# A graph layer on one core: x + beta divided between GpSimd and VectorE, the destination copy moved to ScalarE, a fused compare

## What is computed

```python
h = jnp.maximum(_layernorm(x, axis=-1), 0.0)
edge_input = jnp.concatenate([h[src], h[dst], edge_features, c[src][:, None], c[dst][:, None]], axis=-1)
messages = jax.nn.silu(edge_input @ mW1 + mb1) @ mW2 + mb2
aggregated = jax.ops.segment_sum(messages, dst, num_segments=n_nodes)
u = jax.nn.silu(jnp.concatenate([h, aggregated, c[:, None]], axis=-1) @ uW1 + ub1)
x = x + _layernorm(h + u @ uW2 + ub2, ln_gamma, ln_beta)     # c is node_vec
```

## Time and profile before

| what | us |
|---|---|
| runs | 715.4, 720.5, 722.17 |
| median | 720.5 |
| the profiled execution, its own time | 722.67 |
| span of its instructions | 720.8 |
| busy: PE, DVE | 630.0 (87%), 642.1 (89%) |
| busy: ACT, POOL | 516.5 (72%), 541.0 (75%) |

### The profile page before, as it was taken

How to read it: one execution, slowest core, us unless ns; L and a number is a source line. 1 busy time by engine, 2 the same in 40 slices (tenths; PEclk the granted TensorE clock), 3 DMA queues, 4 the chain that set the end, 5 groups by cost and what they waited for, 6 DMA issues and landing times.

```text
span 720.8 us, 17511 instructions
## 1 busy us (share of the span) xinstructions
PE 630.0 (87%) x3830; PEld 466.2 (65%) x3830; DVE 642.1 (89%) x3060; ACT 516.5 (72%) x1034; POOL 541.0 (75%) x448
## 2 busy tenths in 40 slices
PE   1468999999999999999998998998998998999981
PEld 0235676766776776766766766766767767767771
DVE  4365699999999999999999999999999999999897
ACT  1546778778877787787787787787788788788630
POOL 7778878888888888888888888888888888881210
PEclk9966999999999999999999999999999999999997
DMA  6445556666666666666765766756666766765231
GB/s 133 111 115 131 151 164 160 186 187 163 180 186 163 190 179 163 189 181 161 194 177 160 204 169 166 202 163 170 199 160 179 196 156 180 198 161 173 87 122 69
DMA packets 119053, 118.54 MB, mean 164 GB/s; under 512 B 48764, under 2 KB 93615, under 8 KB 119010
## 3 DMA queue, kind: packets, MB, share of 16 engines
q1 hardware_dynamic: 104884, 91.41, 43.6%
q0 software_dynamic: 12608, 26.25, 16.4%
q10 hardware_dynamic: 1518, 0.42, 0.3%
HBM read 79.31 MB, written 38.70 MB: 164 GB/s over the span
## 4 chain that ended last, share of the span: by engine, by line
POOL 60%; issue 21%; PE 8%; DVE 6%; ACT 2%; DMA 1%; POOLq 1%; ACTq 0%
POOL ends_in L373 47%; POOL x_beta L393 13%; ACT ends_norm L532 2%; DVE y_out L749 1%; DVE centred L632 1%; PE ps_e L458 1%; PE ps_t L486 1%; PE ps_hid L445 1%; PE ps_hid L447 1%; PE ps_e L457 1%; PE ps_e L456 1%; DVE stats L677 1%; PE ps_t L464 1%; DMA ends_in<-in_rows,end_idx 1%; PE ps_f L490 0%
## 5 line engine op out<-in xcount | busy, mean ns | idle before, releaser
L373 POOL DMA_INDIRECT ends_in<-in_rows,end_idx x392 | 422.6, 1078 | 113.3 <-issue 112.5
L476 PE MATMUL ps_upd<-w_out,hidden_n 128*128 128x128 f32 x784 | 140.4, 284 | 33.6 <-DVE centred L632 31.6
L532 ACT ACTIVATE ends_norm<-ends_in,minus,rstd 128x128 f32<-128x128 f32 x392 | 155.9, 484 | 6.6 <-DVE minus L743 6.6
L532 ACT ACTIVATE x_norm<-x_in,minus,rstd 128x128 f32<-128x128 f32 x392 | 156.0, 488 | 6.3 <-DVE minus L743 6.3
L476 PEld LDWEIGHTS ps_upd<-w_out,hidden_n 128*128 128x128 f32 x784 | 119.4, 192 | 41.9 <-DVE centred L632 26.4
L393 POOL TENSOR_TENSOR x_beta<-x_in,beta_row 128x1024 f32<-128x1024 f32 x49 | 116.0, 2368 | 39.1 <-DVE y_out L749 38.2
L632 DVE SCALAR_TENSOR_TENSOR centred<-ps_upd,y_mean,gamma_row 128x128 f32<-128x128 f32 x392 | 135.0, 347 | 0.1
L447 PEld LDWEIGHTS ps_hid<-match,msg_in 113*128 113x128 f32 x784 | 103.0, 191 | 47.2 <-issue 47.2
L537 ACT ACTIVATE ends_t<-ps_t 128x1024 f32<-128x1024 f32 x49 | 50.2, 1024 | 90.9 <-PE ps_f L490 89.3
L477 PE MATMUL ps_upd<-const_sb,h_t 128*128 128x128 f32 x392 | 107.6, 274 | 0.0
L749 DVE SCALAR_TENSOR_TENSOR y_out<-centred,rstd,x_beta 128x128 f32<-128x128 f32 x392 | 107.1, 348 | 0.0
(11 more groups left out here) (79 smaller groups left out, 885.7 us busy)
## 6 DMA issues: line engine op xcount, KB each, us to landing
x_in<-in_x_steps SPq DMA_DIRECT2D x49, 512.0 KB, 5.2
out<-y_out SPq DMA_DIRECT2D x49, 512.0 KB
msg_in<-msgs SPq DMA_DIRECT2D x392, 56.4 KB
msgs<-msg SPq DMA_DIRECT2D x49, 258.0 KB
ends_in<-in_rows,end_idx POOLq DMA_INDIRECT x392
ends_in<-in_attr SPq DMA_DIRECT2D x49, 64.0 KB
end_idx<-in_ends SPq DMA_DIRECT2D x49, 4.0 KB
match<-in_node_vec SPq DMA_DIRECT2D x49, 4.0 KB
```

The lines of the kernel that those rows point to most:

```text
L373: nc.gpsimd.indirect_dma_start(out=dst, out_offset=None, in_=rows, in_offset=bass.IndirectOffsetOnAxis(ap=end_idx[s.slot][:, t, side:side ...
L476: nc.tensor.matmul(ps_upd[:, cols(j)], hidden_n[:, cols(j)], w_out[:, :], start=j % E_TILES == 0, stop=False)
L532: return nc.scalar.activation(dst, source, function, bias=minus[was][:, c:c + 1], scale=rstd[was][:, c:c + 1])
```

## The change

1. `x_beta` is made in two parts: POOL adds tiles 0 to 4 (128x640), DVE adds tiles 5 to 7 (128x384) in the new `add_beta`, which stands between `rstd` and `minus`. Two semaphores take the place of one; SP and `y_out` wait for both.
2. `place` is gone. `match` is one scalar_tensor_tensor on a row of 1024 running numbers: (iota + block base) compared with the destination. The base is a scalar operand read per partition. `match` now stands behind `minus`, right ahead of `y_out`. The running numbers are 128x1024 in SBUF, loaded once, by a transfer on POOL's queue ahead of the first gather; the 128-column ramp in `consts` goes.
3. The polynomial of the Halley step is factored, so that `root_d` and one waited-for step go: 11 small operations in place of 12. `root_c` is a scalar_tensor_tensor with two tensor inputs in place of a tensor_scalar. The eviction of messages now stands behind `newton_b`.
4. The destination copy is an ACT activation between `hidden_e` and `h_t`.

```diff
+POOL_TILES = 5
...
-                nc.gpsimd.tensor_tensor(x_beta[near.slot][:, :, :], x_in[near.slot][:, :, :],
-                                        beta_row[:, :, :].broadcast_to([P, N_TILES, H]), ALU.add).then_inc(x_beta_ready, 1)
+                nc.gpsimd.tensor_tensor(x_beta[near.slot][:, 0:POOL_TILES, :], x_in[near.slot][:, 0:POOL_TILES, :],
+                                        beta_row[:, :, :].broadcast_to([P, POOL_TILES, H]), ALU.add).then_inc(x_beta_low_ready, 1)
...
+            pool.dma_start(iota[:, :, :].rearrange("p j m -> p (j m)"), iota_row.rearrange("(o n) -> o n", o=1).broadcast_to([P, N_STEP])).then_inc(iota_loaded, 16)
...
+                if own:
+                    act.wait_ge(edge_loaded[own.slot], (own.fills4 + 1) * 16)
+                    wait(act, msg_stored[own.slot], 16 * own.fills4)
+                    nc.scalar.activation(msg[own.slot][:, :, H:H + 1], end_idx[own.slot][:, :, 1:2], ACT.Copy).then_inc(dst_copied, 1)
...
-                    V.tensor_tensor(match[near.half][0:WINDOW, :, :], place[near.half][0:WINDOW, :, :].broadcast_to([WINDOW, N_TILES, P]),
-                                    iota[0:WINDOW, :, :].broadcast_to([WINDOW, N_TILES, P]), ALU.is_equal).then_inc(match_ready, 1)
+                    V.scalar_tensor_tensor(match[near.half][0:WINDOW, :, :], iota[0:WINDOW, :, :],
+                                           const[0:WINDOW, bass.ds(C_BASE + N_TILES * near.n, 1)],
+                                           msg_in[near.half][0:WINDOW, :, H:H + 1].broadcast_to([WINDOW, N_TILES, P]),
+                                           ALU.add, ALU.is_equal).then_inc(match_ready, 1)
...
+                def add_beta():
...
+                    wait(dve, out_ready, near.n - RING + 1)
...
+                    V.tensor_tensor(x_beta[near.slot][:, POOL_TILES:, :], x_in[near.slot][:, POOL_TILES:, :],
+                                    beta_row[:, :, :].broadcast_to([P, N_TILES - POOL_TILES, H]), ALU.add).then_inc(x_beta_high_ready, 1)
...
-                V.tensor_scalar(root_c[:, at], root_b[:, at], 0.375, -1.25, ALU.mult, ALU.add).then_inc(stat_ops, 1)
+                V.scalar_tensor_tensor(root_c[:, at], root_b[:, at], 10.0 / 3.0, root_b[:, at], ALU.subtract, ALU.mult).then_inc(stat_ops, 1)
...
-                V.tensor_tensor(root_d[:, at], root_c[:, at], root_b[:, at], ALU.mult).then_inc(stat_ops, 1)
+                V.scalar_tensor_tensor(halley[:, at], root_c[:, at], 5.0, guess[:, at], ALU.add, ALU.mult).then_inc(stat_ops, 1)
```

More of the change, by code:

```diff
@@ L46 @@
 MAGIC = 0x5F3759DF
-C_IDENT, C_LOWER, C_IOTA = 0, P, 2 * P
-C_BOUND = 3 * P
+C_IDENT, C_LOWER = 0, P
+C_BOUND = 2 * P
 C_SEARCH = C_BOUND + PER_LANE + 1
@@ L143, in gnn_layer @@
 def gnn_layer(nc, rows, x_steps, ends, dst_all, dst_seen, attr, node_vec, mW1, mb1, mW2, mb2, uW1, ub1, uW2, ub2,
-              gamma, beta, consts, out):
+              gamma, beta, consts, iota_row, out):
     f32, bf16, i32 = mybir.dt.float32, mybir.dt.bfloat16, mybir.dt.int32
@@ L203, in gnn_layer @@
         msg_in = [sb(f"msg_in{b}", [P, N_TILES, MSG_ROW]) for b in range(2)]
-        place = [sb(f"place{b}", [P, N_TILES, 1]) for b in range(2)]
+        iota = sb("iota_sb", [P, N_TILES, P])
         match = [sb(f"match{b}", [P, N_TILES, P]) for b in range(2)]
@@ L644, in evict_messages, with match_nodes @@
                                     fold_bias[:, :, :].broadcast_to([P, E_TILES, H]), ALU.add).then_inc(msg_ready, 1)
-                def copy_dst():
-                    if not own:
-                        return
-                    dve.wait_ge(edge_loaded[own.slot], (own.fills4 + 1) * 16)
-                    wait(dve, msg_stored[own.slot], 16 * own.fills4)
-                    V.tensor_copy(msg[own.slot][:, :, H:H + 1], end_idx[own.slot][:, :, 1:2]).then_inc(dst_copied, 1)
-                def place_messages():
+                def match_nodes():
                     if not near:
@@ L688, in body @@
                 if not (new or nxt or prev):
-                    copy_dst()
                     evict_messages()
-                    place_messages()
+                    add_beta()
                     match_nodes()
@@ L733, in body @@
                 evict_messages()
                 dve.wait_ge(stat_ops, base + 11)
-                V.scalar_tensor_tensor(newton_b[:, at], newton_a[:, at], -0.5, var[:, at], ALU.mult, ALU.mult).then_inc(stat_ops, 1)
-                place_messages()
-                dve.wait_ge(stat_ops, base + 12)
                 wait(dve, ends_norm_ready, it.edges_upto(-RING))
                 wait(dve, x_norm_ready, it.nodes_upto(-2))
-                V.scalar_tensor_tensor(rstd[b][:, at], newton_b[:, at], 1.5, halley[:, at], ALU.add, ALU.mult).then_inc(rstd_ready, 1)
@@ L741, in body @@
-                match_nodes()
+                V.scalar_tensor_tensor(rstd[b][:, at], newton_b[:, at], 1.5 * 0.375, halley[:, at], ALU.add, ALU.mult).then_inc(rstd_ready, 1)
+                add_beta()
                 dve.wait_ge(rstd_ready, 2 * it.stats_before() + 1)
                 V.scalar_tensor_tensor(minus[b][:, at], s_add[:, at], -0.5, rstd[b][:, at], ALU.mult, ALU.mult).then_inc(rstd_ready, 1)
+                match_nodes()
                 if prev:
                     dve.wait_ge(centred_ready, 2 * prev.n + 2)
-                    dve.wait_ge(x_beta_ready, prev.n + 1)
+                    dve.wait_ge(x_beta_low_ready, prev.n + 1)
+                    dve.wait_ge(x_beta_high_ready, prev.n + 1)
@@ L812 @@
               "uW1": L0_gnn_uW1, "ub1": L0_gnn_ub1, "uW2": L0_gnn_uW2, "ub2": L0_gnn_ub2,
-              "gamma": L0_gnn_ln_gamma, "beta": L0_gnn_ln_beta, "consts": consts}
+              "gamma": L0_gnn_ln_gamma, "beta": L0_gnn_ln_beta, "consts": consts, "iota": np.arange(N_STEP, dtype=np.float32)}
     nc = bacc.Bacc("TRN2", target_bir_lowering=False, num_devices=1)
```

31 lines of the change are left out of this document (14 added, 17 removed).

## The result

The changed kernel takes 732.9 us (median of 4, 731.1 to 734.5) where the kernel before takes 720.1: a ratio of 1.019, 95% interval 1.013 to 1.024. It is slower by nearly 2%. The interval lies above 1, so the loss is real. The forecast of 717 was wrong; the time is near that of the first rival (736). The profiled execution took 734.5 with a span of 732.5.

A forecast was written before the change was run, and what follows sets the result against it. The prediction took two bounds: a PE and ACT ring (13.2 us a period), then full POOL (13.42). With the ring setting all periods, -6.4 + 0.6 + 0.5 = -5.3 from 722.67 gave 717 us; range 712 to 742 for 8 in 10.

The forecast's parts named there:

- the first rival: DVE's hold on POOL runs through from `match` to the last `y_out`: slower, 736 us, about 775 if most gathers miss; chance 0.36.
- The ring of 13.20: Loop through PE and ACT, without DVE and POOL, claimed to set every one of 42 periods at 13.20 us: -6.4 us.
- POOL 11.42 without stretches: POOL's need per period in us without lengthened gathers, after its x_beta falls from 2.36 to 1.50.
- DVE: DVE's work per period: +0.18 us in sum, 12.85 without its wait for gathers, under the ring's 13.20.
- What POOL does in its spare time: POOL's add waits for `y_out`, so POOL rests there while `y_out` holds it up anyway; lengthened gathers cost nothing.
- the large stretch: The gather on POOL that takes 1.90 us in place of 0.95, held until 0.83 after the last `y_out`.
- The rival's price: A hold of 3.4 us costs POOL 2.15 to 3.4 a period; period taken as 13.7, +12.6 over 42 periods.
- The toss-up: Whether POOL's sixth gather slips in ahead of `match` or behind `add_beta` (13.6 us a period) or misses it (14.7).
- The dearer case: The sixth gather misses getting in ahead of `match`: periods of 14.7 us, about 775 in all; chance 0.05.
- ACT's copy: The destination copy on ACT fits the 0.52 us gap before `h_t`: cost 0, 0.12 left; rival 726 us, chance 0.05.
- Start and end: Ahead of the steady periods +0.6 us for one more load on POOL's queue; last iterations +0.5 us on DVE.
- The sum: All terms for the whole kernel: -6.4 + 0.6 + 0.5 = -5.3 us, from 722.67 to 717.4.

The follow-up runs named there:

- Kind 8: In a kernel without the layer: `match` directly ahead of eight `y_out` with two already met waits between; the gather ended 0.82 us after the last `y_out`.
- the good kernels: Changed kernel with `minus` between `match` and `y_out`, 714.8 us; kernel before with a 24-column copy inside `y_out`, 715.9; kernel before with x_beta's division alone, 716.3.
- The pairs: Kernel without the layer: POOL issues gathers, DVE runs 12 kinds of `match` then eight `y_out`, 9 times each; gathers came through between them in 54 of 108.
- the kernel with the order alone changed: Kernel before, loop in three stretches: `minus` ahead of `match`; as it was; a 24-column copy inside `y_out`. 745.1 us, ratio 1.034.
- the kernel with three stretches: Changed kernel, loop in three: as changed; old compare directly ahead of `y_out`; fused compare with `minus` between it and `y_out`. 727.5 us, ratio 1.009.
- kind 5: In a kernel without the layer: `match` directly ahead of eight `y_out` with a constant scalar; no gather came through between `match` and `y_out`.

## Why the prediction was wrong

- **The ring of 13.20**: right. The first six periods of the changed kernel have a mean of 13.18; with `minus` between, 36 of 42 are 13.18 to 13.20.
- **POOL 11.42 without stretches**: right. `x_beta` took 1.55, not 1.50; the period without stretches comes to 11.46.
- **DVE**: `add_beta` 0.47 from start to start (0.46 expected), the fused `match` 405.31 - 404.11 = 1.20 against 1.15, so +0.05 for +0.08. DVE did not set the period.
- **The step that failed** is "What POOL does in its spare time": that the large stretch falls into time that is free. It rested on a gather coming through between `match` and `y_out`, so that one period holds POOL for about one `y_out` row. The argument against the rival was that waits for semaphores between the two may open the gap. Kind 8 shows that met waits don't. What the runs showed in its place: the seventh gather, held through to the end of the last `y_out`, takes 2.99 to 3.09 us in nearly every period, so that POOL mostly needs 13.6 to 13.9, over the ring. The trace of before held the pattern already: between `match` and `minus` a gather came through each time (43 of 43), between one `y_out` and the next never (0 of 41). What was missing was to ask what distinguishes the two places, and a short operation between long ones does. Nor was POOL's spare time there in the kernel where the time came out as forecast: with `minus` between, it has no idle time ahead of `x_beta` from 186 to 582 us. A chance of 0.36 was too low for the only pattern that the rows showed.
- **The rival's price**: right in kind and size. It decides from a stretch of 1.78 us; measured 2.04 + 0.11. Settled period 13.7 worked out, 13.68 measured; 573.4 us for 42 periods, 572.8 measured. That the totals lie so near is partly luck: seven periods went by, not four, before PE felt it, and two dearer ones (14.14, 16.41), of which 1.6 us are the clock's, made up for it. The start and end added by the rival (+1.1) did not come.
- **The toss-up** at 8 us into the period (the terms given add up to 8.03, not 8.05) fell as taken: in the steady part the sixth gather came through ahead of `match`, mostly at the end of `add_beta`. The dearer case was seen three times, at 117.10, 610.13 and 637.83 (3.98, 3.63 and 3.64 us). The one at 610.13 began 0.55 us into `match`; the period behind it is the 16.41, lengthened by the clock as well.
- **ACT's copy**: right, nothing. The ACT timeline of the changed kernel:

```profile
127.36 0.20 ACT L560 ACTIVATE msg<-end_idx 128x4 f32<-128x4 int32 x1
127.88 1.11 ACT L564 ACTIVATE h_t<-ps_t,b_col 128x1024 f32<-128x1024 f32 x1 [0.32 <-PE ps_t L467]
```

  `h_t` still waits 0.32 for PE; 0.12 of room was expected.
- **Start and end**: +0.6 and +0.5 were expected; the steady part begins 0.4 earlier and the end is the same. The start differs by 2.6 us among the good kernels (91.5 to 94.1), so a term of 0.6 cannot be read there.
- **The sum** holds once the hold is cut: 717 forecast, 714.8 measured with `minus` between.

The Trainium skill's page "SBUF — State Buffer", section "Who interferes with whom", says that an instruction holds the pair to its end. The pairs agree with a hold for a whole instruction (0.82 us from its end to the gather's), but not that the loser is let in at each end: in 54 of 54 pairs of `match` and a large instruction it was not, while behind `add_beta` it was, 18 of 18 times, with `match` next. The page's rule fits the one place and not the other.

## What to carry to other kernels

Where GpSimd issues gathers beside VectorE, look for unbroken rows of large two-tensor operations, not for single ones: here a gather that met `match` and the eight `y_out` waited for all of them. Read from the trace which neighbours join, for not all do. Before operations are moved, look at which short one stands between long ones; it may be where the other engine gets in. If none is there, a copy of 24 columns for 0.09 us may pay, as it did here (5 us of 721). And where a trace shows the same thing each time in one place and never in another, weigh that above a reason that one has only thought of.

## What the runs showed of the hardware that I had not expected

- Between `match` and `y_out` a held gather gets in at a two-tensor operation of 24 columns, a copy, or statistics of PSUM (54 of 54); a wait that is met does not let it in (9 of 9). Between `add_beta` and `match` it gets in with nothing between them (18 of 18). Two exceptions were seen. In the second stretch of the kernel with the order alone changed, a gather that began at 382.65 came in between two of the eight `y_out`. The other was in the kernel with three stretches: a gather that began at 226.10 inside `add_beta` was not let in at the `minus` behind it and took 4.56 us, to 0.8 after the last `y_out`. Why is open for both.
- Eight `y_out` in a row with a constant scalar take 1.70 us (kind 5), with a per-partition one 2.18; a 112x1024 compare with a constant scalar 1.204, with a per-partition one 1.265. The scalar costs about 0.06 us an instruction at both sizes.
